# MLP weight chunks rounded on ScalarE instead of GpSimd, with a new order of steps on four engines

## What is computed

```
sa, ca, ga, sb, cb, gb = silu(c) @ wmod                   # per sample, 6 x 256
h = layernorm(x) * (1 + ca) + sa
x = x + floor(ga) * attn(h)                               # floor: sign kept, |g| >= 0.25
h = layernorm(x) * (1 + cb) + sb
return x + floor(gb) * moe(h)

attn(x): h = layernorm(x); xc = silu(conv4(h))
  q, k = l2norm(h @ Wq), l2norm(h @ Wk);  v = layernorm(h @ Wv)      # 16 heads of 16
  u = sigmoid(xc @ Wig + big) * k * v;  g = sigmoid(xc @ Wg + bg)
  mem[t] = g[t] * mem[t-1] + u[t]
  out = groupnorm(layernorm(mem) * q) * sigmoid(xc @ Wog + bog)
  h = x + out @ Wo;  h2 = layernorm(h)
  return h + silu(h2 @ Wgate) * (h2 @ Wval) @ Wout                   # the MLP, FF = 1024
moe(x): 16 experts of 176 by top-4 of a softmax, and a shared expert of 352
```

## Time and profile before

| what | value |
|---|---|
| runs shown | 385.27, 385.52 and 614.99 us, median 385.52 us |
| the profiled execution, its own time | 385.01 us |
| its span, first to last instruction | 383.2 us |
| mean granted TensorE clock | 0.993 of full speed |
| busy: PE, DVE, ACT, POOL | 368.9, 245.5, 200.2, 111.0 us |
| DMA | 34.81 MB, mean 91 GB/s |

### The profile page before, as it was taken

The page is one execution under the profiler, slowest core; times in us unless marked ns, Lnnn a source line. Parts: engine busy times, 40 slices in busy tenths (PEclk is TensorE's granted clock), DMA queues, the critical chain, the costliest instruction groups (busy, mean ns, idle before and its releaser), DMA issues.

```text
span 383.2 us, 4573 instructions
## 1 busy us (share of the span) xinstructions
PE 368.9 (96%) x1590; PEld 286.2 (75%) x1590; DVE 245.5 (64%) x439; ACT 200.2 (52%) x314; POOL 111.0 (29%) x94
## 2 busy tenths in 40 slices
PE   6997988999999999999999999999999999999995
...
DMA packets 18967, 34.81 MB, mean 91 GB/s; under 512 B 2528, under 2 KB 6496, under 8 KB 18944
## 3 DMA queue, kind: packets, MB, share of 16 engines
...
HBM read 33.39 MB, written 1.11 MB: 90 GB/s over the span
## 4 chain that ended last, share of the span: by engine, by line
PE 83%; DVE 7%; ACT 4%; DMA 2%; SPq 2%; issue 1%; POOL 0%; DVEq 0%; ACTq 0%
PE ps L1399 12%; PE ps L1401 12%; PE ps L1400 12%; PE ps L1432 6%; PE ps L1436 6%; PE ps L1433 6%; PE ps L1351 4%; PE ps L1356 4%; PE ps L1352 4%; PE ps L1117 3%; PE ps L1134 3%; PE ps L1118 3%; DMA w<-in_wsm 2%; DVE w L857 1%; PE ps L1303 1%
## 5 line engine op out<-in xcount | busy, mean ns | idle before, releaser
L372 POOL TENSOR_TENSOR wsm_lo<-w,wsm_hi 128x768 fp32r<-128x768 f32 (+1 forms) x40 | 71.2, 1784 | 204.1 <-ACT wsm_hi L694 183.2
L1399 PE MATMUL ps<-b_hi,wsm_hi 128*128 128x512 f32 x200 | 79.3, 396 | 0.0
L1401 PE MATMUL ps<-b_lo,wsm_hi 128*128 128x512 f32 x200 | 78.9, 395 | 0.0
L1400 PE MATMUL ps<-b_hi,wsm_lo 128*128 128x512 f32 x200 | 78.9, 395 | 0.0
L706 ACT ACTIVATE a_hi<-w 128x512 fp32r<-128x512 f32 x50 | 31.6, 632 | 86.4 <-DVE w L1060 83.5
L1056 DVE TENSOR_TENSOR w<-w,gate_b 128x512 f32<-128x512 f32 x44 | 43.1, 980 | 41.6 <-ACT w L700 41.6
L1065 DVE TENSOR_TENSOR a_lo<-w,a_hi 128x512 fp32r<-128x512 f32 x50 | 34.6, 693 | 31.6 <-ACT a_hi L706 31.5
L700 ACT ACTIVATE w<-ps 128x512 f32<-128x512 f32 x50 | 29.9, 597 | 34.7 <-PE ps L1401 34.6
L1399 PEld LDWEIGHTS ps<-b_hi,wsm_hi 128*128 128x128 f32 x200 | 37.7, 188 | 8.9 <-POOL wsm_lo L372 0.2
L1401 PEld LDWEIGHTS ps<-b_lo,wsm_hi 128*128 128x128 f32 x200 | 37.7, 188 | 8.9
L1400 PEld LDWEIGHTS ps<-b_hi,wsm_lo 128*128 128x128 f32 x200 | 37.7, 188 | 8.5
...
## 6 DMA issues: line engine op xcount, KB each, us to landing
...
stage<-in_wff SPq DMA_DIRECT2D x4, 512.0 KB, 6.5
...
w<-in_wsm SPq DMA_DIRECT2D x3, 512.0 KB, 9.1
w<-in_x SPq DMA_DIRECT2D x3, 512.0 KB, 3.6
...
```

Of the source, the lines that this page charges most:

```text
L372: return nc.gpsimd.tensor_tensor(lo, raw, f32(hi), ALU.subtract)
L1399: mm(bank, mgu(wsm_hi, slot, k, which), b_hi[b][:, k, :], start=k == 0, stop=False)
L1400: mm(bank, mgu(wsm_lo, slot, k, which), b_hi[b][:, k, :], start=False, stop=False)
L1401: last = mm(bank, mgu(wsm_hi, slot, k, which), b_lo[b][:, k, :], start=False, stop=k == KC - 1)
```

## The change

The function bodies stay as they are; only the four plans change. All six `chunkhi` steps leave POOL_PLAN, and six `chunk` steps enter SCALAR_PLAN. With that, the order of steps is a new one on all four engines. The core of the diff:

```diff
 TENSOR_PLAN = """
-    ones warm.2 scale shift.0 gate.0 shift.1 chan t1.0.0 t1.0.1 gate.1 q.0 qlo.0 k.0 klo.0 v.0 ig.0 iglo.0 ssk.0 ssv.0
-    ga.0 t1.1.2 u.0 og.0 mem.0 q.1 qlo.1 oc.0 k.1 klo.1 vo.0 v.1 wo.0 ig.1 tw.0 iglo.1 ga.1 ssk.1 t2.0 og.1 ssv.1
-    up.0.0 u.1 up.0.1 up.0.2 mem.1 up.0.3 oc.1 down.0.0 vo.1 down.0.1 up.0.4 wo.1 down.0.2 tw.1 down.0.3 up.0.5 up.0.6
-    down.0.4 t2.1 up.0.7 down.0.5 up.1.0 down.0.6 down.0.7 up.1.1 tm.0 up.1.2 down.1.0 up.1.3 down.1.1 down.1.2 up.1.4
-    t3.0 up.1.5 down.1.3 up.1.6 logits.0 down.1.4 down.1.5 up.1.7 wt.0 down.1.6 down.1.7 eup.0.0 tm.1 eup.0.1 eup.0.2
-    edown.0.0 edown.0.1 eup.0.3 edown.0.2 eup.0.4 t3.1 eup.0.5 edown.0.3 eup.0.6 logits.1 edown.0.4 eup.0.7 edown.0.5
-    edown.0.6 wt.1
+    warm.2 ones scale shift.0 shift.1 gate.0 gate.1 t1.0.0 t1.0.1 chan k.0 q.0 qlo.0 klo.0 ig.0 iglo.0 ssk.0 v.0 ssv.0
+    ga.0 t1.1.2 u.0 og.0 mem.0 q.1 qlo.1 oc.0 vo.0 k.1 klo.1 v.1 wo.0 ig.1 iglo.1 tw.0 ga.1 ssk.1 t2.0 ssv.1 og.1
+    up.0.0 u.1 up.0.1 up.0.2 down.0.0 mem.1 down.0.1 up.0.3 oc.1 up.0.4 vo.1 down.0.2 up.0.5 wo.1 down.0.3 tw.1 up.0.6
+    down.0.4 down.0.5 down.0.6 t2.1 up.0.7 up.1.0 up.1.1 down.0.7 up.1.2 down.1.0 tm.0 up.1.3 down.1.1 up.1.4 down.1.2
+    up.1.5 down.1.3 t3.0 down.1.4 up.1.6 logits.0 up.1.7 down.1.5 wt.0 down.1.6 eup.0.0 eup.0.1 down.1.7 edown.0.0
+    eup.0.2 tm.1 eup.0.3 edown.0.1 edown.0.2 eup.0.4 edown.0.3 eup.0.5 t3.1 edown.0.4 eup.0.6 logits.1 edown.0.5
+    eup.0.7 wt.1 edown.0.6
 """
 SCALAR_PLAN = """
-    rstd.0.0.0 gate.0 rstd.0.0.1 rstd.0.1.0 shift.1 rstd.0.1.1 wsm.0 wsm.1 wsm.2 h1hi.0.0 h1hi.0.1 h1.0.0 h1.0.1 gate.1
-    wsm.3 wsm.4 q.0 xconv.0 sqk.0 sqv.0 ig.0 rk.0 rv.0 ga.0 wsm.5 h1hi.1.0 h1hi.1.1 h1.1.0 h1.1.1 sqm.0 og.0 rm.0 q.1
-    sqo.0 k.1 wsm.6 ro.0 v.1 gated.0 xconv.1 wo.0 ig.1 ga.1 rk.1 h2hi.0.0 h2hi.0.1 h2.0.0 h2.0.1 rv.1 silu.0.0 og.1
+    rstd.0.0.0 rstd.0.0.1 gate.0 rstd.0.1.0 rstd.0.1.1 wsm.0 gate.1 wsm.1 h1hi.0.0 h1.0.0 h1hi.0.1 wsm.2 h1.0.1 chunk.0
+    wsm.3 shift.1 chunk.1 xconv.0 q.0 sqk.0 wsm.4 ig.0 rk.0 sqv.0 wsm.5 rv.0 ga.0 h1hi.1.0 h1hi.1.1 h1.1.0 h1.1.1 sqm.0
+    og.0 rm.0 q.1 chunk.2 sqo.0 chunk.3 wsm.6 ro.0 k.1 gated.0 v.1 xconv.1 chunk.4 wo.0 chunk.5 ig.1 ga.1 rk.1 h2hi.0.0
+    h2hi.0.1 h2.0.0 h2.0.1 rv.1 silu.0.0 silu.0.1 hid.0.0 og.1 silu.0.2 hid.0.1 sqm.1 rm.1 hid.0.2 silu.0.3 hid.0.3
+    sqo.1 silu.0.4 ro.1 gated.1 silu.0.5 wo.1 hid.0.4 ehigh.0.0 hid.0.5 ehigh.0.1 silu.0.6 hid.0.6 h2hi.1.0 h2hi.1.1
...
 VECTOR_PLAN = """
...
-    modc var0.1.2 h1lo.0.0 h1lo.0.1 conv.0.0 conv.0.1 xlo.0.0 xlo.0.1 scaled0.1.2 shifted.1.2 var1.1.2 a1.0 uk.0
+    vsum conv.0.0 h1lo.0.0 h1lo.0.1 modc conv.0.1 scaled0.1.2 xlo.0.0 xlo.0.1 shifted.1.2 var1.1.2 a1.0 uk.0 hn1.1.2
...
+    hidlo.0.2 prod.0.3 hidlo.0.3 sqe.1 prod.0.4 osig.1 gated.1 outlo.1 prod.0.5 modg.1 hidlo.0.4 wo.1 var2.1 hidlo.0.5
+    prod.0.6 hn2.1 hidlo.0.6 h2lo.1 prod.0.7 prod.1.0 hidlo.0.7 hidlo.1.0 prod.1.1 hidlo.1.1 prod.1.2 sum3.0 prod.1.3
+    gated3.0 plus_x.0 hidlo.1.2 var3.0 hidlo.1.3 prod.1.4 hn3.0 prod.1.5 hidlo.1.4 gbc prod.1.6 hidlo.1.5 hidlo.1.6
+    lgsub.0 topk.0 h3lo.0 prod.1.7 wt.0 hidlo.1.7 egated.0.0 elo.0.0 egated.0.1 elo.0.1 egated.0.2 sum3.1 gated3.1
...
 POOL_PLAN = """
-    wsm.0 wsm.1 wsm.2 vcentre wsm.3 chunkhi.0 wsm.4 chunk.0 chunkhi.1 rstd.1.0 rstd.1.1 chunkhi.2 wsm.5 chunk.1 chunk.2
-    sqq.0 chunkhi.3 chunkhi.4 chunk.3 wsm.6 chunk.4 sqv.1 chunkhi.5 chunk.5 sqq.1 sqk.1 rstd.0.2 rstd.1.2 elow.0
-    rstd.0.3 elow.1 elow.2 elow.3 elow.4 rstd.1.3 elow.5 elow.6 elow.7
+    wsm.0 wsm.1 vcentre wsm.2 chunk.0 rstd.1.0 wsm.3 wsm.4 sqq.0 rstd.1.1 wsm.5 chunk.1 wsm.6 sqq.1 chunk.2 chunk.3
+    sqk.1 sqv.1 chunk.4 chunk.5 rstd.0.2 elow.0 elow.1 rstd.1.2 rstd.0.3 elow.2 elow.3 elow.4 elow.5 rstd.1.3 elow.6
+    elow.7
 """
```

More of the change, by code:

```diff
@@ L97 @@
-    ehigh.0.4 esilu.0.3 ehid.0.3 ehigh.0.5 esilu.0.4 ehigh.0.6 h3.1 esilu.0.5 esilu.0.6 ehid.0.4 ehigh.0.7 ehid.0.5
-    exp.1 ehid.0.6 esilu.0.7 ehigh.0.8 ehid.0.7 ehigh.0.9
+    rstd.0.0.0 rstd.0.0.1 gate.0 rstd.0.1.0 rstd.0.1.1 wsm.0 gate.1 wsm.1 h1hi.0.0 h1.0.0 h1hi.0.1 wsm.2 h1.0.1 chunk.0
+    wsm.3 shift.1 chunk.1 xconv.0 q.0 sqk.0 wsm.4 ig.0 rk.0 sqv.0 wsm.5 rv.0 ga.0 h1hi.1.0 h1hi.1.1 h1.1.0 h1.1.1 sqm.0
+    og.0 rm.0 q.1 chunk.2 sqo.0 chunk.3 wsm.6 ro.0 k.1 gated.0 v.1 xconv.1 chunk.4 wo.0 chunk.5 ig.1 ga.1 rk.1 h2hi.0.0
```

18 lines of the change are left out of this document (9 added, 9 removed).

## The result

| | kernel before | changed kernel |
|---|---|---|
| median of 9 runs each | 388.19 us (385.27 to 614.99) | 390.27 us (389.42 to 392.09) |
| ratio to before, 95% interval | | 1.0093 [1.0067, 1.0119] |
| the profiled execution's own time | 385.01 us | 389.57 us |
| its span | 383.2 us | 387.8 us |
| mean granted TensorE clock | 0.993 | 0.989 |

The changed kernel is slower by 0.9%. That is under the 2% that count as a difference, but its interval lies wholly above 1. The ratio is the figure to trust: the runs of the kernel before fall into two groups (385.3 to 386.2 and 388.2 to 388.5, with one of 614.99 apart), and a median of nine can land in either. A second job with the same changed kernel gave 390.13 us against 385.75, ratio 1.0109 [1.0082, 1.0136].

A forecast was written before the change was run, and what follows sets the result against it. PE was taken as the bound from about 85 us, with ACT and DVE chains opening gaps before that. The profiled 385.0 + 1.4 + 0.7 + 0.7 + 0.4 gave 388.2 us, range 382.5 to 391.7.

The forecast's parts named there:

- I take 0: Before 65 us, removing POOL's casts frees no DVE time, as DVE mostly reads PSUM; 0 of up to 6.2 us.
- (2): Routing of sample 0: fewer matmuls between logits.0 and wt.0 to hide topk; 0.7 us, bounds 0 and 1.5.
- (3): Routing of sample 1: 4.2 us of matmuls between logits.1 and wt.1, formerly 7.0; 0.4 us, bounds 0 and 1.
- The copies: Six chunk copies on ACT in place of POOL casts, 1.04 us each, 6.2 us more on ACT.
- The wait for chunk 0: ACT waits for chunk 0 until 19.9 us, opening a PE gap before q.0 of some 2.6 us; charged nothing.
- wo.0's lateness: wo.0 on ACT starts at 68.4 against 65.52 us, +2.9, of which 1.04 is chunk 4.
- To u.1, +1.4 us: From the front to u.1, ACT's and PE's new order makes PE finish u.1 1.4 us later; bounds -2.7 and +2.9.
- (1) down.0.6, 0.7 us: After u.1, PE waits for down.0.6's low part, behind hn2.1, rstd.1.2 and two elows; 0.7 us, bounds 0 and 1.8.
- A: Rival: not slower, the order refills the front; -1.3 to -2.5 us, 382.5; chance 0.28.
- B: Rival: the lower clock lasts over q.0, qlo.0 and klo.0, +2.9 us to iglo.0 and after, 391.1; chance 0.10.
- C: Rival: chunk transfers become the bound, chunk 4 lands late ahead of wo.0; +5.9 us, 394.1; chance 0.07.

The follow-up runs named there:

- a0: The changed kernel itself, unaltered, run again as the base for most comparisons; 390.13 us.
- e14: Changed kernel with three POOL holds: chunk 1's low part behind hn1.1.2, elow.0 behind hn2.1 (rstd.1.2 first), elow.2 behind hn3.0; 388.16 us, 1.0059.
- e5: Changed kernel with POOL's rstd.1.2 ahead of elow.0 and elow.1 again; 394.24 us, 1.0198.
- e11: Changed kernel with POOL's rstd.1.2 ahead of elow.0 and elow.1, and elow.0 held until DVE's hn2.1 is done; 389.62 us, 1.0095.
- e13: Kernel before, old order, with the six chunk copies on ACT and low parts placed out of DVE's way, chunk.4 behind sqm.1; 386.21 us, 1.0012.
- e12: Changed kernel with wsm.3 and shift.1 ahead of chunk.0 on ACT; 391.1 us, 1.0128.
- e3: Changed kernel with chunks 4 and 5 copied later on ACT, behind silu.0.0, and rstd.0.2 ahead of their low parts on POOL; 392.0 us, 1.0158.
- e4: Changed kernel with POOL's low part of chunk 1 held until DVE's hn1.1.2 is done; 388.82 us, 1.0078.
- e10: Changed kernel with chunk 1's low part, elow.0 (rstd.1.2 first) and elow.2 held on POOL, and tw.0 ahead of iglo.1 on PE; 388.56 us, 1.0062.
- e7: Changed kernel with POOL's sqq.0 and the low parts of wsm.5 and chunk 1 held until DVE's hn1.1.2 is done; 390.04 us, 1.009.

## Where the prediction failed, and what in it held

**The step that failed** is the term put at nothing, "I take 0": what POOL's work does to DVE. In its place the runs show 2.0 us, 390.13 in a0 against 388.16 in e14 with the low parts held out of the way, and 4.6 us where two meet hn2.1 (e5 against e11). The terms (2) and (3) failed as well: 1.1 us in the sum, 0.2 at most in the runs. That e14 stands at the forecast's 388.2 is in part luck: of its 1.8 us after u.1 only 0.45 is a gap that was foreseen.

**The copies.** Right in length, 1.06 us each, and by e13 free of cost on a chain that has room. The wait for chunk 0 in the new order shows no cost either (e12). Of wo.0's lateness the prediction gave 1.04 us to chunk 4; the copy did delay wo.0 by about that, but not t2.0 (e3).

**To u.1, +1.4 us.** The term of ACT's and PE's order had the right size: with the collisions taken away (e14) u.1 is late by 1.3, in e4 by 1.2. Its path is less sure: e10 brings t2.0 0.7 us earlier and u.1 not at all. And that ACT's times fit within 0.7 us is luck, as they hold 1.2 us of collision; without it ro.0, wo.0 and h2hi.0 start at 55.38, 67.78 and 77.49 (e14), 0.5 to 0.8 earlier than worked out. The changed kernel has +2.5. What failed is the step that stands ahead of the sum: "I take 0: at the casts' times (before 65 us) DVE mostly reads PSUM". It asked only what goes away with the casts. It did not ask what the **moved low parts** would stand beside. Chunk 1's low part went from 42.2 us, beside the scan, to 37.5, beside hn1.1.2, and cost 1.15 us there (e4); POOL worked 2.25 us between 30 and 40 us before, 7.5 after. Nor was it so that DVE mostly reads PSUM there: L805 and L764 do not. I also took only half of a condition, the two SBUF inputs, and L764, with one tensor input, would have looked safe by that half. The full rule (the Trainium skill, GPSIMD Engine Reference, Key points) names a DVE instruction in a 2-port mode or with two SBUF inputs. By the Trainium skill (VectorE: DVE Perf Modes, Mode 2×_2P) that mode is for instructions such as a `tensor_scalar` from SBUF to SBUF. L764 is one, and the runs agree: 1.38 us alone, 4.38 in e5.

**(1) down.0.6, 0.7 us.** The size came out (0.69), the cause only in part: 0.26 from the elows, 0.45 that stays without them (e11). Taken by itself the reason would mislead, for the repair that it suggests is e5, the worst version of the new order on ACT.

**(2) and (3) routing, 0.7 and 0.4 us.** Wrong, the measured gap is none (0.2 us at the first expert tile). The working has a slip, 4.9 less 1.2 is 3.7 and not 3.9, which makes the first term 0.5 instead of 0.7. More to the point, I had worked with topk as it ran before. Its last step took 1.03 us at 158.05 beside an elow; in the changed kernel it took 0.23 (timeline of DVE):

```profile
163.24 0.23 DVE L1037 SCALAR_TENSOR_TENSOR wres<-rep,sc 128x64 f32<-128x64 f32 x1
```

From lgsub (160.14) to its end topk took 3.3 us and not 3.9. A duration taken from the trace held a collision that the new order removed. plus_x.0 is the same (2.32, now 1.23). In their place stands a gap of 0.48 at t3.0, where elow.2 now meets hn3.0.

**Rivals.** A (the order refills the front) fell: ro.0 came early as it says, but wo.0 did not start before 65.5. B: the slow stretch did lengthen, to 6.8 us,

```profile
17.40:24.20 6.80, 6.80 (x19) 5.27 (x19) 6.59 (x13) 6.27 (x10) 5.82 (x7) 0.50 0.29 106
```

over k.0 and most of q.0 (windows of the changed kernel; the clock is the last but two), but ig.0's gate on ACT still came at 29.23 us, where it was 29.84 before. The stretch only used up slack: PE, without a pause since 18.12, reached iglo.0's low part at 28.51, when DVE had it ready (26.86 to 28.13). Where the stretch lay later (a0, e3, e7, e11) the gate came at 30.3 to 30.9: there B is right in kind, with 1.1 to 1.6 us for its 2.9, and I had given it too little as a part of every outcome. C did not happen; chunk 4's load took 3.7 us and chunk 5's 5.7, with 0.5 us of waiting.

**The sum.** Forecast 1.4 + 0.7 + 0.7 + 0.4 = 3.2. Measured 2.5 to u.1 (1.3 order, 1.2 collision or late clock) and 2.1 after it (0.69 and 0.48 as gaps, 0.2 at the experts, about 0.3 in the slower starts behind them; 0.4 not resolved). The errors have opposite signs, 1.1 us of routing too much and the collisions left out, so the total looks better than the argument was.
